# Macaron block in float32r: matmul operands streamed from the last column to the first, and the weights moved by 256 bytes in SBUF

## The reference, cut to what matters

```
def ffn(x):                                   # D_IN 128, D_HID 512
    h = silu(x @ w1.T * w1_s) * (x @ w2.T * w2_s)
    h = gelu(h @ h1.T * h1_s)
    h = gelu(h @ h2.T * h2_s)
    return h @ w3.T * w3_s

def attn(x):                                  # 16 states, 512 steps
    xB = x @ B;  h_t = tanh(xB_t + h_(t-1) @ A.T)
    return (h @ C) @ W_out.T + b_out

x = x + 0.5 * ffn(layernorm(x))
x = x + attn(layernorm(x))
x = x + 0.5 * ffn(layernorm(x))
```

## Time and profile before

| | us |
|---|---|
| median of 3 runs | 384.68 |
| lowest and highest | 384.30, 384.71 |
| the profiled execution | 385.06 |
| its span, first to last instruction | 383.1 |

### The profile page before, as it was taken

How to read it: one execution, slowest core, us unless ns; L and a number is a source line. 1 busy time by engine, 2 the same in 40 slices (tenths; PEclk the granted TensorE clock), 3 DMA queues, 4 the chain that set the end, 5 groups by cost and what they waited for, 6 DMA issues and landing times.

```text
span 383.1 us, 6587 instructions
## 1 busy us (share of the span) xinstructions
PE 376.4 (98%) x1793; PEld 300.2 (78%) x1793; DVE 279.7 (73%) x724; ACT 268.0 (70%) x625; POOL 163.9 (43%) x156
## 2 busy tenths in 40 slices
PE   8999999999999999999999999999999999999995
PEld 6777777778878787878778788888888888887774
DVE  4878989896777677576868866776767677686713
ACT  3889595777858688576784767758576775757654
POOL 3555262655525355142551633525334352533421
PEclk9999999999999999999999999999999999999999
DMA  7920000000000000000001001010100101000001
GB/s 226 436 110 1 27 2 27 3 2 28 2 28 0 2 27 0 28 2 28 27 2 56 2 8 49 0 55 2 41 14 0 55 0 55 0 30 26 2 28 32
DMA packets 6365, 14.00 MB, mean 37 GB/s; under 512 B 1088, under 2 KB 2112, under 8 KB 6080
## 3 DMA queue, kind: packets, MB, share of 16 engines
q1 hardware_dynamic: 5328, 13.37, 9.1%
q10 hardware_dynamic: 1008, 0.29, 0.3%
HBM read 7.37 MB, written 2.10 MB: 25 GB/s over the span
## 4 chain that ended last, share of the span: by engine, by line
PE 85%; issue 7%; POOL 3%; ACT 3%; DVE 2%; POOLq 0%; DVEq 0%
PE F L274 66%; PE FR L274 7%; PE SC L491 2%; PE FR L302 2%; POOL y_lo L1489 1%; PE SC L422 1%; POOL y_lo L1495 1%; PE F L519 1%; ACT y_hi L1216 1%; PE FR L292 1%; PE SC L274 1%; PE MI L302 1%; ACT y L1213 1%; PE F L521 1%; PE MI L282 1%
## 5 line engine op out<-in xcount | busy, mean ns | idle before, releaser
L274 PE MATMUL F<-y_hi,w_hi 128*128 128x512 f32 (+1 forms) x484 | 196.6, 407 | 0.3 <-DVE y_lo L1045 0.2
L274 PE MATMUL F<-y_lo,w_hi 128*128 128x512 f32 (+1 forms) x484 | 188.6, 390 | 0.0
L274 PEld LDWEIGHTS F<-y_hi,w_hi 128*128 128x128 f32 x484 | 90.9, 188 | 20.7 <-issue 2.2
L1213 ACT ACTIVATE y<-F,sc 128x512 f32<-128x512 f32 x111 | 76.1, 686 | 41.3 <-PE F L274 40.1
L274 PEld LDWEIGHTS F<-y_lo,w_hi 128*128 128x128 f32 x484 | 91.2, 188 | 15.9
L837 DVE TENSOR_TENSOR y_lo<-y,y_hi 128x512 fp32r<-128x512 f32 x79 | 64.8, 821 | 39.2 <-ACT y_hi L1216 39.2
L1489 POOL TENSOR_TENSOR y_lo<-y,y_hi 128x512 fp32r<-128x512 f32 x48 | 66.7, 1398 | 59.1 <-DVE y_hi L824 48.5
L1495 POOL TENSOR_TENSOR y_lo<-y,y_hi 128x512 fp32r<-128x512 f32 x48 | 62.6, 1310 | 34.6 <-ACT y_hi L1216 34.4
L1216 ACT ACTIVATE y_hi<-F,sc 128x512 fp32r<-128x512 f32 x111 | 76.1, 685 | 0.0
L1232 ACT ACTIVATE h<-SC 128x32 fp32r<-128x32 f32 x96 | 18.8, 196 | 48.0 <-PE SC L437 46.8
L274 PE MATMUL F<-xn_hi,w_hi 128*128 128x512 f32 x118 | 49.5, 419 | 0.1
(11 more groups left out here) (170 smaller groups left out, 439.6 us busy)
## 6 DMA issues: line engine op xcount, KB each, us to landing
x_all<-in_xT SPq DMA_DIRECT2D x1, 2048.0 KB, 16.1
x_all<-x1c SPq DMA_DIRECT2D x8, 256.0 KB, 2.3
x_all<-lnin SPq DMA_DIRECT2D x8, 256.0 KB, 2.2
out<-outb SPq DMA_DIRECT2D x7, 256.0 KB, 2.0
x_all<-in_xtok SPq DMA_DIRECT2D x1, 1536.0 KB, 12.0
w_raw<-in_h1T SPq DMA_DIRECT2D x2, 512.0 KB, 7.8
w_raw<-in_h2T SPq DMA_DIRECT2D x2, 512.0 KB, 9.3
x_all<-in_xtok SPq DMA_DIRECT2D x2, 128.0 KB, 3.2
```

The source lines that it names most:

```text
L274: mm = nc.tensor.matmul(out, wtile(w, layer, k, m), y, start=first and i == 0, stop=last and i == len(pairs) - 1)
L1213: nc.scalar.activation(y23[:, m, :], bankt[:, :], ACT.Gelu, scale=s)
```

## The change

The diff has four edits. (1) `gap` grows from 136 to 200 columns of 4 bytes, and a new unused `gap2` of 448 columns stands behind the three weight tensors: `w_raw`, `w_hi` and `w_lo` move by 256 bytes, and all behind them by 256 + 1,792 = 2,048 bytes. (2) `back(t)` gives a view of t with its columns from last to first, and every main matmul streams such a view. Its output is then stored mirrored; four layers mirror four times, so the end is in the usual order. (3) In `last_layer4` the half of the columns that a part writes is the mirror of the half that it streams (`mirrored`). (4) The two output halves of the last chunk leave in the other order. The transposes, `x_times_b`, `scan_step`, `attention` and `zeros` are as before.

```diff
-        gap = sb("gap", [P, 136])
+        gap = sb("gap", [P, 200])
         w_raw = sb("w_raw", [P, WOFF[5]])
         w_hi = sb("w_hi", [P, WOFF[5]], F32R)
         w_lo = sb("w_lo", [P, WOFF[5]], F32R)
+        gap2 = sb("gap2", [P, 448])
...
+        def back(t):
+
+            return t[:, ::-1]
+
+        def mirrored(half):
+
+            return slice((1 - half) * HCOLS, (2 - half) * HCOLS)
...
-                    mm = nc.tensor.matmul(out, wtile(w, layer, k, m), y, start=first and i == 0,
+                    mm = nc.tensor.matmul(out, wtile(w, layer, k, m), back(y), start=first and i == 0,
...
-                        mm = split_mm(B4_LAST[half][:, cut], 4, k, 0, y3_hi[:, k, cut], y3_lo[:, k, cut], k == 0, k == KT - 1, gen)
+                        mm = split_mm(B4_LAST[half][:, mirrored(half)], 4, k, 0, y3_hi[:, k, cut], y3_lo[:, k, cut], k == 0, k == KT - 1, gen)
...
-                cut = slice(half * HCOLS, (half + 1) * HCOLS)
+                cut = mirrored(half)
...
-                sp.dma_start(outT[:, k * N:k * N + HCOLS], outb[:, 0:HCOLS]).then_inc(out_half, 16)
+                sp.dma_start(outT[:, k * N + HCOLS:(k + 1) * N], outb[:, HCOLS:N]).then_inc(out_half, 16)
                 sp.wait_ge(l4_out, gb + k + CHUNKS + 1)
-                sp.dma_start(outT[:, k * N + HCOLS:(k + 1) * N], outb[:, HCOLS:N]).then_inc(out_sem, 16)
+                sp.dma_start(outT[:, k * N:k * N + HCOLS], outb[:, 0:HCOLS]).then_inc(out_sem, 16)
```

More of the change, by code:

```diff
@@ L499, in first_layer1 @@
                 for b in range(2):
-                    nc.tensor.matmul(out[b][:, :], w[b][0], xn_hi[:, :], start=True, stop=False)
+                    nc.tensor.matmul(out[b][:, :], w[b][0], back(xn_hi), start=True, stop=False)
                 pe.wait_ge(w_lo1_ready, 1)
                 for b in range(2):
-                    nc.tensor.matmul(out[b][:, :], w[b][1], xn_hi[:, :], start=False, stop=False)
+                    nc.tensor.matmul(out[b][:, :], w[b][1], back(xn_hi), start=False, stop=False)
                 pe.wait_ge(xn_lo_r, 1)
                 for b in range(2):
-                    nc.tensor.matmul(out[b][:, :], w[b][0], xn_lo[:, :], start=False, stop=False)
-                    mm = nc.tensor.matmul(out[b][:, :], w[b][1], xn_lo[:, :], start=False, stop=True)
+                    nc.tensor.matmul(out[b][:, :], w[b][0], back(xn_lo), start=False, stop=False)
+                    mm = nc.tensor.matmul(out[b][:, :], w[b][1], back(xn_lo), start=False, stop=True)
                 mm.then_inc(l1_mm, 1)
@@ L518, in first_layer2 @@
                     w = wtile(w_hi, 2, k, m)
-                    nc.tensor.matmul(B2[m][:, :], w, y1_hi[:, k, :], start=k == 0, stop=False)
+                    nc.tensor.matmul(B2[m][:, :], w, back(y1_hi[:, k, :]), start=k == 0, stop=False)
                     if k < KT - 1:
-                        nc.tensor.matmul(B2[m][:, :], w, y1_lo[:, k, :], start=False, stop=False)
+                        nc.tensor.matmul(B2[m][:, :], w, back(y1_lo[:, k, :]), start=False, stop=False)
             def first_layer3(y, gen, *pairs):
@@ L527, in first_layer3 @@
                     low = y is y2_lo
-                    mm = nc.tensor.matmul(B3_FIRST[m][:, :], w, y[:, k, :], start=k == 0 and not low,
+                    mm = nc.tensor.matmul(B3_FIRST[m][:, :], w, back(y[:, k, :]), start=k == 0 and not low,
                                           stop=k == KT - 1 and low and not gen)
                     if gen:
-                        mm = nc.tensor.matmul(B3_FIRST[m][:, :], wtile(w_lo, 3, k, m), y[:, k, :], start=False,
+                        mm = nc.tensor.matmul(B3_FIRST[m][:, :], wtile(w_lo, 3, k, m), back(y[:, k, :]), start=False,
                                               stop=k == KT - 1 and low)
@@ L543, in first_turn @@
                             w = wtile(w_lo, 2, k, m)
-                            nc.tensor.matmul(B2[m][:, :], w, y1_hi[:, k, :], start=False, stop=False)
-                            nc.tensor.matmul(B2[m][:, :], w, y1_lo[:, k, :], start=False, stop=False)
-                    nc.tensor.matmul(B2[m][:, :], wtile(w_hi, 2, KT - 1, m), y1_lo[:, KT - 1, :], start=False,
+                            nc.tensor.matmul(B2[m][:, :], w, back(y1_hi[:, k, :]), start=False, stop=False)
+                            nc.tensor.matmul(B2[m][:, :], w, back(y1_lo[:, k, :]), start=False, stop=False)
+                    nc.tensor.matmul(B2[m][:, :], wtile(w_hi, 2, KT - 1, m), back(y1_lo[:, KT - 1, :]), start=False,
                                      stop=True).then_inc(l2_mm, 1)
```

## The result

| | before | after |
|---|---|---|
| median of 4 runs, us | 384.49 | 388.00 |
| lowest and highest | 383.80, 384.71 | 387.49, 388.51 |
| profiled execution, and its span | 385.06, 383.1 | 388.51, 386.6 |

The kernel before has one run more here than in the table ahead of the prediction. The changed kernel is slower: ratio 1.0095, 95% interval 1.0075 to 1.0114, 3.5 us. I had forecast 4 us less.

The account below looks back on a forecast made before the run. TensorE's queue was taken to bound the kernel. Shorter main matmul distances gave 4.1 us less and the other parts zero: 384.68 - 4.1 = 380.6, rounded to 380.5 us, range 368.5 to 389.

Parts of the forecast that it names:

- what bounds the kernel: TensorE's queue sets the time from 10 us to the end, its pace read from start to start of matmuls.
- (2) to (4): Last layer's mirrored halves, swapped output transfers and moved tensors: zero each, bounds +-0.1, +-0.4 and +-0.5 us.
- I take 226.3 ns, close to this even pace: Main matmuls of 512 columns: mean distance from 229.6 to 226.3 ns; the even-pace case had chance 0.34.
- the term of 4.1 us less: Weights 256 bytes on with reversed streams, priced together: 1,255 main matmul distances, each 3.3 ns shorter.
- the even state: Main matmuls at 226 to 227 ns, a state that 646 of the 1,255 distances (at most 228) already had.
- the order of the distances behind a break: Main matmuls: 229, 233, 236, 224, 231, 236, 228, 232, 231, then 227 on, the same for tiles 512 bytes apart.
- the slow pair: Two main matmul distances, 142.82 to 143.29 us, 235 ns each; at worst everywhere, 6.8 us more.
- an extra of 13 to 22 ns per main matmul: Time on top of the columns' 213.5 ns: 13 in the even stretch, 22 in the slow pair, 16 on average.
- it goes with the weight load: The main matmuls' extra does not grow with columns; it comes with the one weight load per matmul.
- PE and ACT never wait on anyone: Rule of two independent TensorE read ports: addresses and direction change nothing, and the time stays.
- The slower rival: Every main matmul: reads keep in step and always meet, 5.4 ns each, 391.5 us, half of it 388; chance 0.26.
- Nothing moves: Main matmuls: the extra is a constant of the weight change, addresses do not touch the order; 384.7 us; chance 0.15.

Follow-up runs that it names:

- pieces turned: The kernel before with the reversed order by 256-byte pieces, forward inside a piece, the other edits kept, weights on a multiple of 2,048 bytes: 384.26 us, ratio 1.0005.
- experiment 1: Two kernels: the changed kernel without the 256-byte weight move, 388.27 us, ratio 1.0097; the kernel before with only that move, 384.52 us, ratio 1.0002.
- second set: Separate kernel: groups of 24 matmuls, each behind a 32-column matmul, varying offset, direction, tile width, columns and turned unit; 16-byte units turned 233.3 ns, 256-byte pieces 226.7.
- fourth set: Separate kernel: groups of matmuls at further 16-byte steps of weight offset, forward and reversed, and offsets with narrow tiles; one-column tile 231.1 to 231.8 ns.
- third set: Separate kernel: groups of 24 matmuls with narrower tiles, other column counts, turned units and offsets; one-column tile 231.8 ns forward, 233.3 reversed.
- first set: Separate kernel: groups of matmuls back to back on random data, varying offsets, direction, columns and data type; at 0 bytes 226.7 ns forward, 233.3 reversed.

## Why the prediction was wrong, step by step

**Right: what bounds the kernel.** TensorE's queue, read from distances between starts. Nothing else became late, and the time followed the mean distance in every kernel: 229.6 or 229.8 ns with 384.3 to 384.5 us, 232.2 to 232.9 with 386.9 to 387.4, 233.3 to 233.6 with 388.0 to 388.3.

**Right: the parts that the prediction numbers (2) to (4) cost nothing.** The kernel with pieces turned has the mirrored halves, the swapped transfers and the moved activations, and is at 1.0005; the moved weights by themselves are at 1.0002.

**The step that failed: "I take 226.3 ns, close to this even pace".** The 1,262 distances have a mean of 233.6, so the term of 4.1 us less was 4.9 us more (1,255 x 3.9), of which 1.4 came back: 0.5 at the breaks, as seven distances fewer were long ones, 0.6 in the short matmuls and 0.3 at the start. The order alone gives the whole of it, 233.6 ns in experiment 1. I had argued that the even state "needs no new property of the chip". But whether a stream settles there is a property of its order inside 256 bytes and of the weights' place modulo 256, and no row of before shows a reversed stream. Nor is the order of the distances behind a break as fixed as I wrote: in the trace of before, 45 stretches have ten or more such distances in a row; some begin as I wrote, others enter in the middle and go 236, 228, 233, 231, 226. With no row on the deciding operation, the slow pair's 235 ns was as near as the even 226.6, and I let the more pleasant one win.

**Half right: "an extra of 13 to 22 ns per main matmul", and that "it goes with the weight load".** The size is right, and it is within 12 to 20 ns per matmul from 256 to 512 columns. It is a constant only roughly: 13.3 ns with 256, 320, 384 and 512 columns forward, 16.3 to 16.7 with 448 to 504. That it goes with the reading of weights does not hold: a tile one column wide pays 18 and 20.

**Half right: the rule that "PE and ACT never wait on anyone"** (the Trainium skill, page "SBUF — State Buffer", section "Who interferes with whom"). By it addresses change nothing. That is what 256 bytes did, but for another reason: 256 is a whole period. At 32 bytes the same tiles cost 2.6 us. The measurement decides: where weights and a float32r stream lie towards each other changes the pace.

**The slower rival** named the place (every main matmul) and the price (up to 5.4 ns; 388 us at half of it; measured 388.0), and the time lies in the stated range. That the time matches so well is luck: half the price is 2.7 ns a matmul and 3.9 were measured, and what came back elsewhere made up for it. Its mechanism, two reads kept 256 bytes apart, was not it: the order alone does the same. "Nothing moves" fell for the order, and held for the offset.

**Still open.** Why lines in falling order inside 256 bytes cost 6.7 ns with 512 columns and nothing with 256 and 320, what a 4-byte stream waits for with a tile one column wide, and why a break decides between steady states at 144 bytes. The distance in bytes between weights and stream is not all of it either: weights at 240 and the stream at 0 settled at 226.7 ns, weights at 0 and the stream at 16, the same distance modulo 256, at 231.2. A matmul with no weight load at all was not tried; every one here loads its tile, so a fixed price of the load for 4-byte data remains possible for the reversed streams.

## What to carry to other kernels

Keep a float32r stream rising through memory, at least inside each 256 bytes: [:, ::-1] on the moving operand cost 3 to 4 ns in 230 here with 512 columns (6.7 once settled), and nothing with 256 or 320 columns or in bfloat16. Test an address offset with small steps and remember that it may repeat: two layouts a whole period apart are the same experiment. And a pace that a group shows by itself is only worth taking over if it is reached behind every kind of break that the kernel has.

## What the runs showed of the hardware that I had not expected

- Back-to-back float32r matmuls of 512 columns settle at 226.7 ns forward (weights on a multiple of 256 bytes) and 233.3 reversed; bfloat16 at 215.9 in both directions. With 320 columns float32r has 146.7 in both, with 256 it has 120.0 and 118.8.
- A forward group's settled distance runs from 226.7 to 233.9 ns with the weights' offset modulo 256 bytes (96 bytes: 233.9), a reversed one's from 233.0 to 236.8.
- A matmul's distance depends on the ones before it: 233, 236, 224, 231, 236, 228, 233, 231, then 226.7. The break alone does not fix where a group enters this row: behind the same 32-column matmul, groups with the weights at 0 bytes had eight slow distances (second set), five (fourth set, behind a group at 32 bytes) or two (third set, behind a reversed group).
- Streaming every second column of a 4-byte block costs twice as much: 451 ns for 512 columns (first set).
- With 512 columns forward, a narrower weight tile is slower, not faster: 226.7 ns with 128 columns, 228.9 with 64, 231.6 with 32, 231.8 with one.
